# Taking out the streamed matmuls ahead of the row scores

## The reference

```python
x = _layernorm(x + _L0_attn_ref(x, ...))    # "splat": q, k become exp of distances to 16 centres
x = _layernorm(x + _L0_xattn_ref(x, ctx_512, Wq, Wkv, Wo))          # "cross0": 120 keys
x = _layernorm(x + _L0_ffn_ref(x, router_w, ..., expert_w, ...))    # best of 8 experts
x = _layernorm(x + _L1_attn_ref(x, w_qkv, ..., w_out, ...))         # "causal"
x = _layernorm(x + _L1_xattn_ref(x, ctx_512, ...))  # "self1", "cross1" with heads of 32, each with
                                                    # a gelu layer of 1024 behind it
x = _layernorm(x + _L1_ffn_ref(x, expert_sel, keys, values, route_scale))  # 4 of 16 experts

def attention(q, k, v):      # the form that all five share
    a = softmax(einsum("bqhd,bkhd->bhqk", q, k) * scale, axis=-1)
    return einsum("bhqk,bkhd->bqhd", a, v)
```

## Time and profile before

| what | value |
|---|---|
| three runs | 3750.38, 3753.8, 3755.05 us, median 3753.8 |
| profiled execution | 3753.18 us, its span 3751.0 us |
| granted TensorE clock, mean of the span | 0.924 |
| matmuls (PE) busy | 3123.4 us (83%), 34864 instructions |
| weight loads (PEld) | 2456.7 us (65%) |
| VectorE (DVE) | 2699.4 us (72%) |
| ScalarE (ACT) | 2105.0 us (56%) |
| GpSimd (POOL) | 978.4 us (26%) |

### The profile page before, as it was taken

How to read it: one execution, slowest core, us unless ns; L and a number is a source line. 1 busy time by engine, 2 the same in 40 slices (tenths; PEclk the granted TensorE clock), 3 DMA queues, 4 the chain that set the end, 5 groups by cost and what they waited for, 6 DMA issues and landing times. The chain is left out here.

```text
span 3751.0 us, 89546 instructions
## 1 busy us (share of the span) xinstructions
PE 3123.4 (83%) x34864; PEld 2456.7 (65%) x34864; DVE 2699.4 (72%) x6135; ACT 2105.0 (56%) x4254; POOL 978.4 (26%) x1793
## 2 busy tenths in 40 slices
PE   1989888888888978888988888798988897988886
PEld 1767666766676757766766666676756676766664
DVE  6868676777676767767777667687777677768765
ACT  4745665555556554564565555646655556466542
POOL 1312341122223321231133222212343113124310
PEclk9999899999899989989998988999999999999987
DMA  6211211112112121121121111212121112122110
GB/s 199 70 55 56 79 61 53 45 45 67 55 54 72 48 62 41 50 67 55 48 72 56 54 53 38 70 45 71 60 67 60 39 41 68 48 62 71 60 37 6
DMA packets 362006, 221.49 MB, mean 59 GB/s; under 512 B 102497, under 2 KB 333298, under 8 KB 361586
## 3 DMA queue, kind: packets, MB, share of 16 engines
q1 hardware_dynamic: 361586, 215.76, 19.0%
HBM read 122.23 MB, written 93.32 MB: 57 GB/s over the span
## 5 line engine op out<-in xcount | busy, mean ns | idle before, releaser
L1158 ACT ACTIVATE p<-bank,p_log 128x512 f32<-128x512 f32 (+2 forms) x1280 | 748.3, 585 | 1122.3 <-PE bank L850 1019.3
L1712 POOL TENSOR_TENSOR prob<-p,prob 120x256 f16<-120x256 f32 (+2 forms) x512 | 451.7, 882 | 1650.9 <-ACT prob L1159 1650.5
L1159 ACT ACTIVATE prob<-bank,p_log 128x512 f16<-128x512 f32 (+2 forms) x1280 | 749.3, 585 | 0.0
L1417 DVE TENSOR_REDUCE negm<-bank 128x2 f16<-128x512 f32 (+1 forms) x1280 | 674.8, 568 | 98.9 <-PE bank L813 89.2
L1347 DVE TENSOR_TENSOR prob<-p,prob 128x512 f16<-128x512 f32 (+2 forms) x768 | 485.6, 641 | 92.6 <-ACT prob L1159 88.5
L720 PE MATMUL bank<-w_exp,ident_h 128*128 128x512 f16 x1280 | 418.9, 411 | 101.7 <-DMA k_ring<-k_heads 85.8
L829 PE MATMUL bank<-q_ring,k_ring 80*128 80x256 f16 (+4 forms) x2048 | 445.1, 284 | 40.8 <-ACT raw L1105 14.4
L850 PE MATMUL bank<-ident_h,negm 128*128 128x256 f16 (+2 forms) x2560 | 440.7, 259 | 0.0
L1721 POOL TENSOR_SCALAR_AFFINE_SELECT probm<-prob 128x128 f16<-128x128 f16 x1024 | 326.7, 357 | 308.9 <-DVE prob L1347 308.9
L813 PE MATMUL bank<-k_ring,q_ring 80*128 80x256 f16 (+4 forms) x2560 | 368.5, 259 | 34.8 <-DVE negm L1417 34.2
L813 PEld LDWEIGHTS bank<-k_ring,q_ring 80*128 80x128 f16 (+1 forms) x2560 | 236.5, 104 | 234.2 <-issue 51.5
(11 more groups left out here) (299 smaller groups left out, 6190.1 us busy)
## 6 DMA issues: line engine op xcount, KB each, us to landing
q_ring<-q_heads SPq DMA_DIRECT2D x768, 40.0 KB, 2.2
q_heads<-q_made SPq DMA_DIRECT2D x96, 256.0 KB, 2.4
k_heads<-k_made SPq DMA_DIRECT2D x96, 256.0 KB, 2.3
q_ring<-q_heads SPq DMA_DIRECT2D x512, 48.0 KB, 2.2
k_ring<-k_heads SPq DMA_DIRECT2D x512, 40.0 KB, 2.2
q_heads<-q_made SPq DMA_DIRECT2D x144, 128.0 KB, 1.8
k_heads<-k_made SPq DMA_DIRECT2D x144, 128.0 KB, 1.8
k_ring<-k_heads SPq DMA_DIRECT2D x256, 48.0 KB, 2.2
```

The lines of the kernel that those rows point to most:

```text
L1158: act(p32[0:n, g % PBUF32, 0:cols], ps[0:n, 0:cols], ACT.Exp, bias=p_log[0:n, :], scale=a.scale)
L1159: act(prob[0:n, 0, g % PBUF, 0:cols], ps[0:n, 0:cols], ACT.Exp, bias=p_log[0:n, :], scale=a.scale).then_inc(a_done, one(a_done))
L1417: v.tensor_reduce(negm[:, h * NT:(h + 1) * NT], ring_v[bank_of(e, v_full)][:, :].rearrange("p (t n) -> p t n", t=NT)[:, :, 0:ATTNS[k].keys ...
L1712: g.tensor_tensor(prob[0:n, 1, m % PBUF, 0:cols], p32[0:n, m % PBUF32, 0:cols], prob[0:n, 0, m % PBUF, 0:cols], ALU.subtract).then_inc(pp_ ...
```

## The change

The count of streamed matmuls ahead of the row scores goes from two to zero. `stream` is then called with zero everywhere and issues nothing. All else stays.

```diff
-STREAM_NORM, STREAM_GATES, STREAM_HEADS, STREAM_ROWS = 0, 0, 0, 2
+STREAM_NORM, STREAM_GATES, STREAM_HEADS, STREAM_ROWS = 0, 0, 0, 0
```

## The result

The changed kernel took 3779.81 us (median of 4 runs, 3774.55 to 3788.92) against 3752.59 us before (4 runs). The ratio is 1.0075, 95% interval 1.0054 to 1.0096: 0.75% slower, 28 us by the ratio, where 1.0% faster was forecast. The profiled execution took 3774.55 us, its span 3772.5.

The account below looks back on a forecast made before the run. It took TensorE as busiest (83%) and the largest part of the path, with no engine full. 3753 - 86 (streams off the path) + 47 (lower clock) = 3714 us, 1.0% faster; range 3640 to 3790.

Parts of the forecast that it names:

- Price of the streams: Ahead of the row scores: two streamed matmuls cost 0.49 us a pair, 313 us of TensorE's time over 640 pairs.
- Share on the path: Of the streams' time, 31% lies on the chain of waits: 96 us, less a tenth, so 86 us gained.
- Level of the clock: TensorE's mean clock over the head pairs falls from 0.93 to 0.90, 215 us more at the half clock.
- Price of the half clock: Each microsecond more at TensorE's half clock costs 0.22 us, so 47 us given back.
- rival (a): Stretches the streams kept filled fall to 1.2 GHz and stay; slower if the mean clock is under 0.875; chance 0.28.
- The rule of long idle gaps: TensorE's clock falls in long idle gaps between bursts; by it the clock would not change here, leaving 86 us gained.
- rival (c): TensorE's clock stays at 0.93 and the gain is whole: 3657 us, or 3597 with half on the path; chance 0.20.
- The rule on short idling: Short idling between groups of matmuls also lowers TensorE's clock; it was taken to speak against the change, with no size.

Follow-up runs that it names:

- cols32: The two streamed matmuls for each pair load only 32 columns of weights (128x32 stationary), against the kernel before the change: 3782.51 us, ratio 1.0078.
- rows32: The two streamed matmuls for each pair run over 32 of the array's 128 rows, against the kernel before the change: 3953.18 us, ratio 1.0531.

## Why the prediction was wrong

The measured time lies inside the stated range of 3640 to 3790, but at its slow end and on the wrong side of the kernel before. The terms of the sum, one by one:

- **Price of the streams, 313 us of TensorE's time.** Right as read: 0.43 us for a pair at the full clock.
- **Share on the path, 31%, 86 us gained.** Right. Attention by attention the gain is 85 us (57 to 113), the loose fit over 2, 1 and 0 streams gives 88, and cols32 gives 24 to 31% for time added at the same place. It was read from the last tenth of the kernel, and nothing before the result showed that this part stands for the whole, so that much was luck.
- **Level of the clock, 0.90, "about midway between 0.93 and 0.86".** This step failed. It came to 0.862. 471 us more at the half clock instead of 215. The midpoint had no row behind it, while the earlier trace rows showed that a stretch with 0.59 us of streams kept the clock and its thinner neighbour lost it. A tenth of TensorE's work was taken out of stretches like these all over the kernel, and gave 33 more falls and stays that were a third longer.
- **Price of the half clock, 0.22 us.** Right or a little low: 0.23 (0.18 to 0.27) for this very change, attention by attention, 0.25 by the fit, 0.27 to 0.30 by the rows32 and cols32 pair. With the right level and the forecast's own price the sum is 3753 - 86 + 104 = 3771, already slower. So the level turned the sign by itself. The term that it sizes, 47 us given back, was 104 us by the forecast's price and some 118 by 0.25, which makes 3785; the measured 3780 lies between.
- **The argument against rival (a),** that "at half the speed the remaining work fills TensorE by itself", is shown wrong by the stretch at 1707.20: 8.96 us busy of 13.6 at the half clock. There TensorE stood 4.2 us for VectorE's norm, and half speed does not make work for it.
- **Rival (a)** is what happened: a mean clock under 0.875, and 3777 us at 0.86. Its mechanism, more falls and no quick return, shows in the 129 stays of 8.1 us against 96 of 6.0. It had 0.28.
- **The rule of long idle gaps** (the Trainium skill, TensorE: Matmul & The Clock Gate, section "HAM oscillation — how this bites in real kernels") led to a faster kernel (3657 us in rival (c)) and covers only part of this one. The longest ordinary waits are the same after as before (4.3 us for z, 8.3 and 8.4 us for the ring), but there are more long ones: TensorE's idle gaps of over 3 us went from 26 to 42 by the two traces, and in each of them, or within 4 us behind it, the clock is at half. That much agrees with the rule. But 73 of the 96 falls before, and 86 of the 129 after, have no such gap in the 10 us ahead of them. The rule on short idling (the Trainium skill, the same title, section "A second HAM failure mode: psum-queue depth-cycling") agrees with these.
- That the loss stood in the cross and splat attentions and not in causal and self1 was not forecast at all. The forecast took one clock for the whole kernel.

## What to carry to other kernels

Work that nobody reads can pay when it keeps TensorE's clock at 2.4 GHz, and it has two prices that can be read apart: its share on the path (here a quarter to a third of its time) and the half-clock time that it prevents (here 0.23 to 0.30 us for each microsecond). Before taking any work off TensorE, price the clock as a term of its own, and do not take the middle of two ends for its level. One run with half of the work taken out gives a first reading of how fast the clock falls. After a change, set the traces against each other stage by stage: length against half-clock time gives both prices at once, and the stages that come out shorter are those in which the work cost more than its clock was worth. Put such streams only in the others. A stage's busy share alone does not tell which these are (splat and self1 above).

## What the runs showed of the hardware

- Streams over fewer rows of the array did not hold the clock, streams over fewer columns did. Over 32 of 128 rows they left it at 0.855, under the 0.862 of no streams at all; over 32 of 128 columns they gave 0.924, that of the full ones. Both last the same (0.53 and 0.54 us a pair at the full clock). Only these shapes, and one row with one column (0.840), were run.
- A stream with fewer rows or fewer columns of weights is slower to start and to leave: over all pairs at the full clock the first follows the last matmul by 0.11 us (0.03 before), and the row scores follow the first stream by 0.53 or 0.54 us (0.43 before). The row scores' weight loads (L813) in cols32 stood idle before them at each of the 640 pairs, by the view of that line (us in total, times):

```profile
  issue: 309.9, 640
```

  In the kernel before that was 51.5 us in 190 times. The load no longer runs ahead under the stream: before, it starts with the second stream (2 ns behind it), and in cols32 308 ns behind it, just ahead of its own matmul. The pair takes about 0.19 us more. Why was not tried.
- Each further stream for a pair adds less to the clock: 0.862, 0.898, 0.924 and 0.953 for 0, 1, 2 and 4.
